# Filling the first accumulator ahead of the gates' stores, and alternating the scatters from the first one

## The reference

```
xn  = layernorm(x)
out = x + attention(xn) + moe(xn)

attention: q, k, v by two linear layers each; q, k = elu(.) + 1; 16 heads of 8 channels
           S = sum over tokens of k q^T;  o = v S / (q . k);  y = xn + o Wo + bo
           result = gamma * (y - mean) * rsqrt(var + 0.001) + beta
moe:       shared = (x1 * silu(x2)) W2 of a 384-wide layer, for every token
           gates = softmax(xn Wg) over 64 experts, top 8, renormalised
           each expert: a 384-wide layer of the same form for up to 160 tokens
           combined[token] += gate * expert output
```

## Time and profile before

| | before |
|---|---|
| median of 3 runs (lowest, highest) | 336.98 us (336.37, 337.58) |
| the profiled execution | 336.0 us |
| its span, first to last instruction | 334.2 us |
| PE, DVE, POOL, ACT busy, share of the span | 96%, 79%, 77%, 62% |
| granted TensorE clock | 1.0 of full speed |
| DMA, mean over the span | 213 GB/s |

### The profile page before, as it was taken

One profiled execution on the slowest core, in us unless ns is written; L12 is line 12 of the kernel. 1 busy time (PEld: TensorE's weight loads), 2 busy tenths in 40 slices (PEclk: granted clock), 3 DMA queues, 4 the chain that ended last, 5 costly groups with the idle time before them and its releaser, 6 DMA issues.

```text
span 334.2 us, 9266 instructions
## 1 busy us (share of the span) xinstructions
PE 319.8 (96%) x3059; PEld 305.4 (91%) x3059; DVE 264.4 (79%) x1071; ACT 206.3 (62%) x450; POOL 256.1 (77%) x258
## 2 busy tenths in 40 slices
PE   7999999999999999999999999999999999899974
PEld 7889788899999989999999899999999999899973
DVE  5888998897777769787878798888878775956486
ACT  4889923765757594848476857565686657563210
POOL 6896767468787888778787878878888878888483
PEclk9999999999999999999999999999999999999999
DMA  7999545999787888787878888888887787943798
GB/s 210 333 386 373 152 103 146 297 311 263 162 241 174 235 187 215 177 228 177 220 178 213 187 207 205 198 217 208 204 195 195 191 213 188 242 68 35 153 380 245
DMA packets 60126, 71.15 MB, mean 213 GB/s; under 512 B 14896, under 2 KB 47920, under 8 KB 60080
## 3 DMA queue, kind: packets, MB, share of 16 engines
q1 hardware_dynamic: 42736, 56.47, 54.3%
q0 software_dynamic: 15360, 13.12, 25.0%
q10 hardware_dynamic: 1984, 0.98, 1.0%
HBM read 54.72 MB, written 15.43 MB: 210 GB/s over the span
## 4 chain that ended last, share of the span: by engine, by line
PE 64%; ACT 12%; DVE 10%; issue 5%; DMA 4%; POOL 3%; SPq 1%; DVEq 0%; ACTq 0%; POOLq 0%
PE bank L1431 25%; PE bank L1441 10%; PE bank L1350 7%; PE bank L1364 4%; PE bank L1478 3%; ACT L590 3%; PE bank L1450 2%; PE bank L1502 2%; DMA ew<-acc 2%; POOL acc L545 2%; PE bank L1518 1%; PE bank L1397 1%; PE bank L1484 1%; ACT L593 1%; ACT si L618 1%
## 5 line engine op out<-in xcount | busy, mean ns | idle before, releaser
L545 POOL DMA_INDIRECT acc<-ys,idx_g x64 | 103.4, 1615 | 26.2 <-issue 13.7
L1431 PE MATMUL bank<-xe,ew 128*128 128x160 f32 x768 | 116.1, 300 | 1.8 <-ACT xe L643 1.0
L1431 PEld LDWEIGHTS bank<-xe,ew 128*128 128x128 f32 x768 | 108.4, 190 | 4.4 <-ACT xe L643 1.6
L526 POOL DMA_INDIRECT gath<-xng,idx_g x80 | 81.7, 1022 | 26.3 <-issue 20.1
L618 ACT ACTIVATE si<-bank 128x480 f32<-128x480 f32 (+1 forms) x96 | 52.0, 542 | 59.7 <-PE bank L1431 35.5
L847 DVE TENSOR_TENSOR ac<-si,bank 128x480 f32<-128x480 f32 x64 | 41.7, 652 | 21.6 <-ACT si L618 19.9
L1441 PE MATMUL bank<-ew,ac 128*128 128x128 f32 x384 | 54.9, 279 | 0.0
L1350 PE MATMUL bank<-xT,shw 128*128 128x128 f32 x384 | 50.3, 278 | 0.5 <-ACT si L618 0.5
L1441 PEld LDWEIGHTS bank<-ew,ac 128*128 128x128 f32 x384 | 48.3, 191 | 0.9 <-issue 0.2
L1350 PEld LDWEIGHTS bank<-xT,shw 128*128 128x128 f32 x384 | 46.5, 192 | 1.1 <-issue 0.7
L1364 PE MATMUL bank<-shw,acs 128*128 128x128 f32 x192 | 27.5, 280 | 4.0 <-DVE acs L838 3.0
(11 more groups left out here) (169 smaller groups left out, 568.1 us busy)
## 6 DMA issues: line engine op xcount, KB each, us to landing
ew<-in_expert_w SPq DMA_DIRECT2D x64, 384.0 KB, 3.8
ew<-in_expert_w SPq DMA_DIRECT2D x64, 192.0 KB, 3.4
ew<-acc SPq DMA_DIRECT2D x8, 512.0 KB, 8.2
xng<-xn SPq DMA_DIRECT2D x8, 256.0 KB, 5.4
acc<-zeros SPq DMA_DIRECT2D x4, 512.0 KB, 5.3
acc<-betas SPq DMA_DIRECT2D x4, 512.0 KB, 3.5
x_sb<-in_x SPq DMA_DIRECT2D x7, 256.0 KB, 5.9
gath<-xng,idx_g POOLq DMA_INDIRECT x80, 3.8
```

The costliest lines, as they stand in the source:

```text
L526: pool.indirect_dma_start(out=gath[:, p, m, :], out_offset=None, in_=xng, in_offset=bass.IndirectOffsetOnAxis(ap=idx_g[:, g % 5, m:m + 1], ...
L545: pool.indirect_dma_start(out=acc[adds_to[g, m]], out_offset=bass.IndirectOffsetOnAxis(ap=idx, axis=0), in_=src, in_offset=None, compute_o ...
L1431: last = pe.matmul(h_view(n, half_ + 1, CAP)[:, c, :], ew[p][m][:, k * P:(k + 1) * P], xe[:, p, m, :], start=True, stop=True)
```

## The change

It has two parts. The accumulators now alternate from scatter number 0 on, so (0,0) adds to `acc[0]` and all other scatters stay where they were. And the five fills of `acc[0]` are issued right after the rounds, behind a wait for `betas` alone and ahead of the gates' stores; `counts_in(3)` follows `counts_in(2)` directly. Nothing is added or taken away in computation or in bytes.

```diff
-    adds_to = {u: max(n, 1) % 2 for n, u in enumerate(scatters)}
+    adds_to = {u: n % 2 for n, u in enumerate(scatters)}
...
+            sp.wait_ge(betas_set, 1)
+            for k in range(0, 1024 * N_ACC, 1024):
+                fill(0, k)
             for h in range(len(gated)):
                 gates_store(h)
             cum_store(NR - 1)
             sp.wait_ge(cumB_clear, 16)
             for r in range(NR):
                 sp.wait_ge(cum_out[r], 16)
-            for q in range(1, 3):
+            for q in range(1, 4):
                 counts_in(q)
-            sp.wait_ge(betas_set, 1)
-            for k in range(0, 1024 * N_ACC, 1024):
-                sp.wait_ge(h1_full, up_at['e', 0, min(k // 1024, 2)] + 1)
-                fill(0, k)
-                if k == 0:
-                    counts_in(3)
             for g in range(NG - 1):
```

## The result

| | before | after |
|---|---|---|
| median (lowest, highest) | 337.02 us (336.37, 337.58), 4 runs | 345.03 us (343.94, 348.38), 4 runs |
| the profiled execution, its span | 336.0 us, 334.2 us | 343.94 us, 342.1 us |
| PE, DVE, POOL, ACT busy | 96%, 79%, 77%, 62% | 95%, 77%, 74%, 60% |
| granted TensorE clock | 1.0 | 0.98 |

The ratio is 1.0244 with a 95% interval of 1.0209 to 1.028: 8 us slower. The forecast was 338.1 with a range up to 340.2, so the direction came out and the size did not.

The account below looks back on a forecast made before the run. PE's list was taken to set the pace to about 300 us and POOL's scatters the end; 336.98 us plus 2.8 of stall less 1.7 of POOL's gain, +1.1, gave 338.1 us, range 335.3 to 340.2.

Parts of the forecast that it names:

- The issues alone cost little: On SP, five fill issues of 0.45 to 0.6 us end by about 40.6; the last gates' store waits until 41.6 anyway.
- Landings 4.25 us later: Gates' and count stores, queued behind 5.2 us of fills, land at 48.05 instead of 43.8 us.
- The slack of table(1), 1.3 us: Before table(1) on PE, its counts land near 48.3 and it runs at 49.59; slack 1.3 us, between 0 and 1.6.
- Stall without a fall of the clock: PE idles 2.8 us ahead of table(1), and the forecast adds nothing for a slower clock.
- rival B: At table(1), no slack (shift 4.2 us) and/or a clock fall (1.45 us): 339.5 to 341.0, taken as 340.1; chance 0.15.
- Order of the queue: In SP's queue q1, DMA engines serve descriptors in ring order, so the gates' stores can't overtake the fills.
- Rival A: In SP's queue, the stores are not held back and table(1)'s slack swallows the delay: 335.3 us; chance 0.15.
- and stays there: From the first scatters to the tail, POOL keeps its 1.7 us gain on PE, so the end comes 1.7 us earlier.
- the cap that was worked out: At (1,0) and (3,3), scatters can't start sooner than 0.81 us after their copy, so at most 1.72 us survives.
- a last lag of 3.3: At POOL's last scatter into acc[0], a lag still 3.3 us, not near 1.6, would show part 1 wrong.
- rival C: In the tail, DVE's adds or the 4 MB of reads eat POOL's gain, leaving +2.8 us: 339.8; chance 0.10.
- +2.8: At table(1), PE and everything behind it move 2.8 us later, bounds 2.4 and 4.2.

Follow-up runs that it names:

- e10: Changed kernel with five 8 KB DMAs ahead of the gates' stores instead of the fills, which follow counts_in(3): 338.83 us, ratio 1.0044.
- e9: Changed kernel with four of the five fills issued as one DMA of 2 MB: 345.07 us, ratio 1.0203.
- e14: Changed kernel with 20 useless matmuls on PE ahead of table(1), to keep it busy in the stall: 342.98 us, ratio 1.0138.
- e6: Changed kernel with the five fills issued by ACT in its own queue: 343.55, 343.45, 343.40 and 338.04 us, beside 338.16 for the kernel before.
- e4: Changed kernel with two fills ahead of the gates' stores and three behind counts_in(3): 339.31 us, ratio 1.0041.
- e2: Changed kernel with the fills moved behind counts_in(3), so only the accumulators' alternation is tested: 338.18 us, ratio 1.001.
- e1: Changed kernel with the old order of the accumulators, fills still ahead of the gates' stores: 345.08 us, ratio 1.0218.
- e7: The kernel of e2 without reloading expert weights from group 4 on (8 columns each): 335.76 us, ratio 0.9941.
- e8: Kernel before, without reloading expert weights from group 4 on (8 columns each): 334.85 us, ratio 0.9914.
- e13: The changed kernel itself once more, on one chip with e14: 345.65 us, ratio 1.0235.
- e11: The changed kernel itself once more, on the chip where the kernel before took 355.8 us: 362.58 us, ratio 1.0182.
- e12: Changed kernel with 20 useless matmuls on PE ahead of table(1), on one chip with e11: 365.23 us, ratio 1.0244.

## Why the prediction was wrong

Three terms of the sum failed. The landings of the routing's stores were put 4.25 us later and came 6.1 us later; the clock in the stall was put at nothing and cost 2.87 us; the 1.7 us of part 1 did not reach the end. The slack, the order of the queue and the short waits of POOL at the front came out.

**"The issues alone cost little": wrong.** The argument was that the last gates' store waits for its data until 41.6 in any case. That looks at the last of the four and not at the first two, which used the DMA engines between 38.9 and 41 and now could not. e10 puts a price of at most 1.76 us at table(1) (2.20 - 0.44) and 1.5 at the end on them, with no byte of the fills ahead; it is a bound, since of its delay of 2.95 us only 1.04 are SP's and the rest is the late landing that the kernel after lacks. And with the bytes under way the five issues took 4.36 us instead of e10's 2.50.

**Landings 4.25 us later: mis-sized, 6.1.** The service times were right (fills 38.5 to 44, gates' stores at 280 GB/s against 284). The sum took it that every store is in the queue by the time the DMA engines come to it. SP was held, was done with the last gates' store at 47.52 and with the last count store at 48.35, about when by the sum the count store should have landed (48.05), and counts_in(1) followed 2.1 us behind. e9 shows that it isn't the count of DMAs that holds SP, and that the gap of 47 to 48 is no part of the price.

**The slack of table(1), 1.3 us: right in kind, nearer to 0.8.** 6.1 us later at counts_in(1) gave 4.97 at table(1). Of the 1.1 us between, 0.34 are issues that went faster (1.73 us for the four of cumB instead of 2.07), so that cumL was issued 5.73 us later (52.23 against 46.50), and 0.8 were slack. The first gather, forecast 3.0 us later, came at 51.30 instead of 46.09, 5.2 us later, and kept the order that was forecast: first_rows waits for the table and not for it.

```profile
51.30 1.24 POOL L523 DMA_INDIRECT gath<-xng,idx_g  x1 [7.34 <-issue]
```

**Stall without a fall of the clock: wrong, rival B's mechanism at twice its price.** B had two conditions, no slack and a clock that falls, and priced the second at 1.45 us from the start of the kernel. By the mean clock (0.985 or less) it fell in all 16 runs of the changed kernel, and the price was 2.9 us in the trace (7.72 - 4.85) and 3.3 against e14 (7.76 - 4.42), since PE's work runs at 1.2 GHz for the 8 us from 54 to 62 and does in them what takes 4 to 5 us at full clock. The 7 against 11 matmuls at the start was too mild a measure, and 4 us too short a time. The page "TensorE: Matmul & The Clock Gate", section "Part 1: The HAM clock gate", of the Trainium skill says that an idle TensorE falls to 1.2 GHz; the trace agrees, 0.50 from 52 to 62. The rule stood in the text and was given 0.15, together with the case of no slack. For a stall of the 2.8 us that were forecast the fall should have had a much larger share: in e6 a stall of 2.5 us was followed by it (and three of its four runs have that clock, one has not), in e4 and e10 stalls of 1.9 and 1.6 us were not.

**Order of the queue: right.** The page "DMA: Bandwidth & Descriptors" of the Trainium skill (section "Queues, rings and completion order") says that each DMA engine takes the descriptors of a ring in their order. The trace agrees: 378 GB/s of mostly fills from 38.5 to 44, and the lower rate of the gates' stores, 280, only behind them. Rival A, in which the landings are delayed by less than 3 us, is out.

**Part 1, POOL 1.7 us closer to PE "and stays there": half right.** The mechanism came out at the front: (0,1) 0.30 us behind its gather, the short wait for ACT's copy at (0,3) (1.37 us), a lag of 0.78 at (1,0), the cap that was worked out. (For the lag e2 is the witness, with 0.77; in the kernel after the slow front alone would give it, as e1 says.) "And stays there" failed. It rested on the sentence that the chains of waits behind (0,3) are the same as before. They are the same in the program, but not in time: a POOL that is ahead comes sooner to a scatter whose predecessor lands when it lands, and gives the lead back, 2.5 of 2.7 us in e2's longer other waits. The sign for it had been written down (a last lag of 3.3), and it was 3.58. This is rival C in its result, +0 by part 1, though not by its mechanism: the loads and adds of the tail were not what ate it, the waits on the way were; and e7 beside e8 says that at (15,0) the copies would have taken what was left.

**The sum.** Forecast +2.8 - 1.7 = +1.1. Measured +4.97 (table), +2.87 (clock), 0 (part 1, by e2 and by e1) = +7.84, against +8.0 in the medians. The three errors all lie on one side. The range up to 340.2 held no combination of B with a mis-sized delay.

**What is open.** What exactly holds an issue on SP while fills are under way; why the count store of e4 and e10 lands so late; why POOL's lags in the kernels before and after and in e2 are the same to 0.01 us from (13,2) to (14,0), while e1, under the same traffic, keeps a lead there; how much of the clock's 3.3 us reaches the end, beyond that it is 1.5 to 5.1 us by the intervals of e13 and e14; and why the kernel before takes 355.8 us on one of the chips. None of the kernels that do all of the work is faster than the kernel before.

## What to carry to other kernels

A transfer without a deadline that is put ahead of one with a deadline costs its bytes, its issue time on the engine that issues both, and the time for which later issues are held there while it is under way; on a chain with 1 us of slack all three count. Work out a new stall of TensorE at both clock levels, with the work behind it at half pace until the clock is back, which here raised a loss of 5 us to nearly 8. And a wait that is removed on an engine which isn't last gives time only if nothing on its way to the end waits for the same kind of event: look for the next places where it would arrive early.

## What the runs showed of the hardware

- In a stall of 4.8 us the granted clock of TensorE fell to 0.50 by 52 us and stood there until 62, for 7 to 8 us of that with PE at work again (the kernel after). In e6 a stall of 2.5 us was followed by 0.51 and 0.50 from 54 us on, and two more of its four runs share its mean clock of 0.989 or so. In the traces of e4 and e10, with stalls of 1.9 and 1.6 us, the clock stayed at 1.00 there; no run of theirs has a mean clock under 0.992.
- Six matmuls of 128x160 in float32 took 1.97 us at a granted clock of 0.50 and 1.08 at 1.00 (e13, e14).
- One DMA issue on SP, 0.34 to 0.45 us in a quiet queue, took up to 2.7 us with 2 MB of fills under way (a gates' store of e9, 2.68; its count store, 2.21, which was 0.59 before). Fills in ACT's queue slow SP's issues too (e6: four of 8 KB in 3.62 us instead of 2.07).
- Before a wait for a small store ended, the DMA engines moved only 7 to 13 GB/s in total for 1.5 us (e4, e10).
- The same kernel before took 336.9 to 338.2 us on four chips and 355.8 on a fifth, where in e11 and e12 copies by ACT began after 3.77 and 4.95 us of idling with no releaser on this core.
